# Macaron block with delta-rule attention, one core: sums of squares as TensorE products, and one mixture branch weighted by ScalarE

## The chip, the cores and the metric

One core of a Trainium2 chip. The metric is the device time of one execution in microseconds; the median of three runs of the kernel before is 1182.75 us. Engines: TensorE (PE; its weight loads are listed as PEld), VectorE (DVE), ScalarE (ACT), GpSimd (POOL), SyncE (SP, which issues all the DMAs). A "bank" is one of the eight banks of PSUM, each 128 x 512 f32.

## The reference

Eight sequences of 512 tokens and 256 channels go through half a feed-forward layer, an attention block and half a feed-forward layer again. The change touches the attention: the l2 norms of q and k, and the mixture of four branches.

```python
q = silu(conv(x @ Wq)); k = silu(conv(x @ Wk)); v = silu(conv(x @ Wv))   # 4 heads of 64
beta = sigmoid(x @ Wb)
q, k = q * rsqrt(sum(q*q) + 1e-6), k * rsqrt(sum(k*k) + 1e-6)            # per token and head
# per chunk of 32 tokens: A = -tril(beta k k^T, -1), T = (1 - A)^-1, u = T (beta v), w = T (beta k)
# chunk after chunk: u_i = u - w S; o_i = q S + tril(q k^T) u_i; S += k^T u_i
branches = [fir3(v), fir31(v), delta_o, v]
w = floor_and_renormalise(softmax(gate(x, branches)))                    # 4 weights per token and head
o = sum(w[..., b] * branches[b] for b in range(4))
o = o * rsqrt(mean(o*o) + 1e-5) * onorm_w
x = x + o @ Wo
```

## The kernel before, in words

All work for one sequence is a front part (first feed-forward, projections, convolutions, norms, the inverse T) and a back part (chunk recurrence, gate, mixture, output product, second feed-forward). The kernel is a row of passes that runs the back part of sequence i beside the front part of sequence i+1: one "head" pass (front only), six "body" passes, one "last" pass (like a body without the layernorm of a further sequence) and one "tail" pass (back only). So seven passes hold both parts, eight hold a mixture, and eight hold k and q norms. Each engine has one list of instructions, written out by hand; in a pass, `at.front` and `at.back` pick the parts. Within an engine the order is fixed, so an instruction that waits holds everything behind it.

PSUM banks are handed around by hand. `ORDER` lists, for each kind of pass, which content uses which bank and in which order. TensorE's `claim` waits until the content before in that bank has been given back (`emptied`), the reader's `arrive` waits until the bank is filled, and a reader gives the bank back by raising `emptied`. VectorE's `link` waits for its own instruction, since a later one reads the result.

The steps that the change touches, in the order of a pass:

- ScalarE makes k's two halves by `silu(2)`, `silu(3)` (L632), into `qk_fm` (channels on the partitions). TensorE turns them into banks 0 and 1 (`to_tok`, content `k_t`, L1176). ScalarE squares the two banks into `sq` (L738). VectorE's `k_rows` sums the squares over each head's 64 channels (L1598), adds 1e-6 (L1599), and ScalarE takes the root (L740). Behind the root in ScalarE's list stand `tap(4)`, the four gate gelus (L636), `tap(5)`, the copy of the logits, the copies of k and of the hidden product, and the exponential of the logits (L755).
- TensorE's list after the k transposes: 128 small gram products (`k_products`, L1068, banks 7 and 2), the rest of the q projection, the hidden product, the logit products (L1188), FIR products of the first two heads (`firs(at, 0, ...)`, L1113), the q transposes (`q_t`, banks 3 and 5, L1202), the FIR products of the other two heads.
- ScalarE, after the exponential: `silu(4)`, `silu(5)` (q), copies of the first two FIR banks, the squares of the two q banks (L763), which then are given back.
- VectorE, after the exponential: the mixing weights `mix_w` (L1681 to L1689), then the mixture in place. `f_tok` holds the two FIR branches of a unit (a token tile and head) side by side, `dv_tok` the delta output (slot 0) and v (slot 1). `weighted` multiplies a half of the units, 128 x 1024 elements, by their weights (L1695, four times); `branch_sum` adds `dv_tok` to `f_tok` (L1701, twice), `mixed` adds the two slots (L1706, twice).
- Then the root mean square of the mixed rows: ScalarE squares (L587), VectorE sums (L1711), ScalarE takes the root (L593), VectorE normalises (`mix_normalise`, L1718). TensorE turns the mixed rows (`mixed_rows`, content `mix_t`, banks 6 and 4), with the last FIR products and the v transposes (`v_t`, banks 3 and 5, L1228) between its two halves, then the output product, with the turns of the FIR rows (`fir_rows`) between its halves.
- VectorE after `mix_normalise(1)`: `low_rows(3, "mix_t", 0)` (L1402, the low part of the first mixed rows, which waits for TensorE's turn and ScalarE's high part), `q_rows` (the sum of q's squares, L1617, and the add, L1618), `low_rows(3, "mix_t", 1)`, then the residuals (L1724) and the third layernorm (L1735), whose rows TensorE waits for before the second feed-forward.

The order of the banks that matters here: bank 4 holds the turned beta (`beta_t`) and later the logits, bank 3 in turn a q projection, `q_t`, `v_t`.

## Time and profile before

| | us |
|---|---|
| median of three runs | 1182.75 |
| lowest and highest run | 1180.84, 1190.8 |
| the profiled execution | 1176.66 |
| its span, first to last instruction | 1174.9 |
| TensorE busy | 1051.7 (90%) |
| VectorE busy | 827.4 (70%) |
| ScalarE busy | 551.9 (47%) |
| GpSimd busy | 410.6 (35%) |

The rows further down come from the page and the trace of the profiled execution. A row of a timeline or chain begins with the start in us from the span's start and the time that the row covers; "x8" counts the instructions merged in it; a bracket gives the idle time before and who ended it. A merged row's time runs from the first start to the last end. The ends of matmuls are modelled.

### The profile page before, as it was taken

What the parts mean: (1) busy time and instruction counts of PE and PEld (TensorE: products, weight loads), DVE (VectorE), ACT (ScalarE), POOL (GpSimd) and SP (SyncE); (2) the same over time, 40 slices, a digit from 0 to 9 for tenths busy, and PEclk for the clock granted to TensorE, in tenths of its full rate; (3) what the DMA queues carried; (4) which work ended last, traced back from release to release, by engine and by line L of the source; (5) the groups of instructions that cost most, each with busy time, mean ns of one, the idle gap of its engine ahead of it and who ended that gap; (6) DMA issues with size and microseconds to landing.
All of it is one profiled execution on the core that took longest, in us unless ns stands there. A gap on an engine that the chain in (4) does not pass through costs nothing.

```text
span 1174.9 us, 25682 instructions
## 1 busy us (share of the span) xinstructions
PE 1051.7 (90%) x10348; PEld 785.6 (67%) x10348; DVE 827.4 (70%) x1620; ACT 551.9 (47%) x989; POOL 410.6 (35%) x648
## 2 busy tenths in 40 slices
PE   5858899899999999899998998899998999897738
PEld 4734785588637885488747885488747885486427
DVE  6584478875887668875887668875887668863373
ACT  2254348443564337533575337533574337542431
POOL 7228200951058200961048300771038300770000
PEclk9779799999998999999999999999998999995779
DMA  5140104020130203110140202110040202210000
GB/s 159 20 108 1 37 19 106 4 54 2 51 77 11 45 19 86 24 36 20 33 95 1 55 19 67 42 36 20 28 99 1 54 1 64 46 36 19 1 0 19
DMA packets 82933, 47.45 MB, mean 40 GB/s; under 512 B 58496, under 2 KB 76416, under 8 KB 82816
## 3 DMA queue, kind: packets, MB, share of 16 engines
q1 hardware_dynamic: 82816, 45.82, 16.8%
q8 instruction: 82, 1.34, 0.5%
q14 instruction: 35, 0.29, 0.1%
HBM read 31.12 MB, written 14.68 MB: 39 GB/s over the span
## 4 chain that ended last, share of the span: by engine, by line
PE 69%; DVE 16%; ACT 8%; POOL 3%; issue 3%; DMA 1%; SPq 0%; DVEq 0%; ACTq 0%; POOLq 0%
PE psum L814 14%; PE psum L815 13%; PE psum L816 13%; PE psum L845 6%; DVE arena L1695 4%; PE psum L1007 3%; PE psum L992 3%; PE psum L1026 3%; PE psum L1031 2%; DVE arena L1701 2%; DVE arena L1735 2%; PE psum L1081 2%; PE psum L1188 2%; POOL l_prod L526 1%; POOL arena L530 1%
## 5 line engine op out<-in xcount | busy, mean ns | idle before, releaser
L526 POOL TENSOR_TENSOR l_prod<-arena 64x30 f32<-64x30 f32 (+14 forms) x240 | 143.9, 600 | 547.1 <-DMA arena<-l_dram 528.9
L601 ACT ACTIVATE h_f<-psum,b_col 128x512 f32<-128x512 f32 x128 | 88.1, 688 | 211.7 <-PE psum L816 211.5
L530 POOL TENSOR_TENSOR arena<-arena,l_prod 64x30 f32<-64x30 f32 (+14 forms) x240 | 157.7, 657 | 18.8
L814 PE MATMUL psum<-w_hi,h_hi 128*128 128x256 f32 x512 | 150.4, 294 | 0.0
L1113 PE MATMUL psum<-v_shift,fir_w 128*32 128x512 f32 x1152 | 135.5, 601 | 10.7 <-DVE fir_w L1300 10.7
L815 PE MATMUL psum<-w_lo,h_hi 128*128 128x256 f32 x512 | 144.1, 281 | 0.0
L816 PE MATMUL psum<-w_hi,h_lo 128*128 128x256 f32 x512 | 144.0, 281 | 0.0
L1409 DVE CAST h_hi<-h_f 128x512 fp32r<-128x512 f32 x128 | 63.1, 493 | 86.8 <-ACT h_f L601 43.4
L814 PE MATMUL psum<-xt_hi,w_hi 128*128 128x512 f32 x256 | 113.1, 442 | 7.5 <-DVEq L1396 5.4
L1436 DVE SCALAR_TENSOR_TENSOR conv_acc<-psum,conv_col,conv_acc 128x511 f32<-128x511 f32 x144 | 106.8, 748 | 14.6 <-ACT conv_acc L626 10.9
L845 PE MATMUL psum<-ident,arena 128*128 128x128 f32 x384 | 59.7, 302 | 57.5 <-DVE arena L1735 25.8
L1410 DVE TENSOR_TENSOR h_lo<-h_f,h_hi 128x512 fp32r<-128x512 f32 x128 | 104.9, 820 | 4.4
L815 PE MATMUL psum<-xt_lo,w_hi 128*128 128x512 f32 x256 | 105.9, 414 | 0.0
L816 PE MATMUL psum<-xt_hi,w_lo 128*128 128x512 f32 x256 | 105.2, 411 | 0.0
L814 PEld LDWEIGHTS psum<-w_hi,h_hi 128*128 128x128 f32 x512 | 97.0, 189 | 4.4
L815 PEld LDWEIGHTS psum<-w_lo,h_hi 128*128 128x128 f32 x512 | 97.2, 190 | 2.4
L816 PEld LDWEIGHTS psum<-w_hi,h_lo 128*128 128x128 f32 x512 | 97.0, 189 | 0.0
L845 PEld LDWEIGHTS psum<-ident,arena 128*128 128x128 f32 x384 | 46.9, 153 | 74.2 <-DVE arena L1735 29.5
L1113 PEld LDWEIGHTS psum<-v_shift,fir_w 128*32 128x32 f32 x1152 | 36.7, 111 | 87.8 <-issue 75.8
L814 PEld LDWEIGHTS psum<-xt_hi,w_hi 128*128 128x128 f32 x256 | 51.5, 201 | 20.8 <-issue 10.2
L1485 DVE TENSOR_TENSOR arena<-psum,inv 128x128 f32<-128x128 f32 x64 | 15.6, 285 | 67.4 <-PE psum L1007 67.4
L816 PEld LDWEIGHTS psum<-xt_hi,w_lo 128*128 128x128 f32 x256 | 51.4, 201 | 12.5
(228 smaller groups left out, 2216.3 us busy)
## 6 DMA issues: line engine op xcount, KB each, us to landing
x_in<-in_L_attn_x SPq DMA_DIRECT2D x8, 512.0 KB, 3.9
v_dram<-v_fm SPq DMA_DIRECT2D x16, 256.0 KB, 3.7
v_shift<-v_dram SPq DMA_DIRECT2D x16, 256.0 KB, 3.5
out<-x_tok SPq DMA_DIRECT2D x8, 512.0 KB, 2.8
v_shift<-v_dram SPq DMA_DIRECT2D x16, 255.5 KB, 4.3
v_shift<-v_dram SPq DMA_DIRECT2D x16, 255.0 KB, 5.1
v_shift<-v_dram SPq DMA_DIRECT2D x16, 254.5 KB, 5.7
arena<-in_L_ffn_w SPq DMA_DIRECT2D x2, 1024.0 KB, 7.2
```

Source lines behind the costliest of these rows:

```text
L526: pool.tensor_tensor(prod, l_inv[:, k + 1:, k:k + 1].broadcast_to(shape), l_inv[:, k:k + 1, 0:k].broadcast_to(shape), ALU.mult).then_inc(i ...
L530: pool.tensor_tensor(l_inv[:, k + 1:, 0:k], l_inv[:, k + 1:, 0:k], prod, ALU.add).then_inc(inverted, 1)
L601: act.activation(h_f[:, m % 2, :], bank, ACT.Gelu, bias=b1_col[:, m:m + 1]).then_inc(read, 1)
L814: pe.matmul(dst, a_hi, b_hi, start=first, stop=False, **kw)
L815: pe.matmul(dst, a_hi, b_lo, start=False, stop=False, **kw)
L816: return pe.matmul(dst, a_lo, b_hi, start=False, stop=last, **kw)
L845: last = pe.transpose(bank[:, P * n:P * n + P], src(n), ident[:, :])
L1113: last = pe.matmul(fir[p][0][col:col + 32, :], fir_w[:, group, n - 1 if n else TAPG, :], v_shift[:, group, at_t:at_t + T], start=(n < 2), ...
L1409: link(dve.tensor_copy(h_hi[:, m % RING, :], h_f[:, m % 2, :]))
L1410: dve.tensor_tensor(h_lo[:, m % RING, :], h_f[:, m % 2, :], h_hi[:, m % RING, :].bitcast(F32), ALU.subtract).then_inc(h_split[f], 1)
L1436: ins = dve.scalar_tensor_tensor(out=acc[:, s:], in0=bank[:, 0:T - s], scalar=w[:, CONV - 1 - s:CONV - s], in1=acc[:, s:], op0=ALU.mult, o ...
L1695: return mark(dve.tensor_tensor(src[:, us, :, :], src[:, us, :, :], mix_w[:, us, s:s + 2].unsqueeze(3).broadcast_to([P, 2 * HEADS, 2, D]), ...
```

## The change

The squares of k are taken from `qk_fm`, before any transpose, and so are the squares of q; a 128 x 2 matrix of ones (`pair_sel`) sums them over each head's channels in products whose weights are the squares, eight for k and eight for q. The k sums go into the free columns of the bank of `beta_t`, behind the gram products; the q sums take the place of the q transposes and go into bank 3. VectorE's two sums of squares fall away. In the mixture VectorE weights `dv_tok`'s slot 0 alone, and ScalarE weights slot 1 (v) in sixteen activations of 128 x 64, eight for each half, ahead of and behind the first two FIR copies; VectorE's `branch_sum` waits for them.

```diff
--- before.py
+++ after.py
@@ -120,6 +120,7 @@
         t_two = v_shift[D:D + CHUNK, 6, 32:WIDE].rearrange("p (u j) -> p u j", j=CHUNK)
         f_fm = sb("f_fm", [P, HEADS, T])
         beta_fm = sb("beta_fm", [32, T])
+        pair_sel = sb("pair_sel", [P, 2])
         rows_tok = sb("rows_tok", [P, 3, UNITS])
         nrm, inv = sb("nrm", [P, 2, UNITS]), sb("inv", [P, 2, UNITS])
         c1, c2n = sb("c1", [P, UNITS]), sb("c2n", [P, UNITS])
@@ -154,7 +155,8 @@
         taps_l = f_fm[:, 0, 0:GROUPS * (LONG + 1)].rearrange("p (g n) -> p g n", g=GROUPS)
         taps_s = f_fm[:, 1, 0:GROUPS * CONV].rearrange("p (g n) -> p g n", g=GROUPS)
         at_flat = at_tok[:, :, :].rearrange("p u i -> p (u i)")
-        q_sq = at_flat[:, 0:TILES * C].rearrange("p (u d) -> p u d", u=UNITS)
+        k_sq = sq[:, :, :]
+        q_sq = at_flat[:, 0:HALVES * T].rearrange("p (h t) -> p h t", h=HALVES)
         stat_sel = at_flat[0:D, 0:4 * BR * P].rearrange("p (b m) -> p b m", m=P)
         mean_sel = v_fm[0:D, 1, 0:2 * P].rearrange("p (a m) -> p a m", a=2)
         stat_all = v_fm[:, 1, 2 * P:4 * P].rearrange("p (a m) -> p a m", a=2)
@@ -179,7 +181,7 @@
         K = [("k", (0, 1)), ("beta", (4,)), ("q", (3, 5)), ("beta_t", (4,)), ("k_t", (0, 1)), ("gram", (7, 2)), ("hidden", (6,))]
         LOGIT = [("logit", (4,)), ("logit_t", (4,))]
         FIR = [("fir", (7, 2, 0, 1))]
-        Q = [("q_t", (3, 5))]
+        Q = [("q_sum", (3,))]
         MIX = [("mix_t", (6, 4)), ("wo", (7, 2))]
         V_T = [("v_t", (3, 5)), ("f_t", (0, 1, 6, 4)), ("lhalf", (3, 5)), ("at0", (7, 2))]
         FFN_C = [("ln3", (6, 4)), ("upc", (0, 4) * (KT // 2)), ("outc", (1, 6))]
@@ -307,6 +309,8 @@
         hm_made = sem("hm_made")
         lshift_made = sem("lshift_made")
         exp_made = sem("exp_made")
+        mix_w_made = sem("mix_w_made")
+        v_weighted = sem("v_weighted")
         mix_made = sem("mix_made")
         mix_squared = sem("mix_squared")
         onrm_made = sem("onrm_made")
@@ -318,8 +322,8 @@
         dve_step = sem("dve_step")
         INV_STEPS = 2 * (CHUNK - 2) + 2
         T_LOADS = CPT + 2 * (CPT - 1)
-        DVE_STEPS = {"head": 43, "body": 78, "last": 73, "tail": 40}
-        CONST_MADE, C_LOADED, SETUP_DVE = 60, 57, 36
+        DVE_STEPS = {"head": 41, "body": 75, "last": 70, "tail": 39}
+        CONST_MADE, C_LOADED, SETUP_DVE = 63, 57, 36
         ZEROED, IDENT_MADE = 5, 7
         SETUP_UP, SETUP_FFN, SETUP_PROJ, SETUP_LARGE, SETUP_FIR = 2, 5, 9, 13, 29
 
@@ -467,7 +471,7 @@
                                     pattern=[[-1, P]], channel_multiplier=1))
             assert made == IDENT_MADE
             for t, v in ((low_strict[:, :], 1.0), (up_incl[:, :], 1.0), (eye32[:, :], 0.0), (x_t[:, :, :], 0.0),
-                         (stat_sel, 0.0), (mean_sel, 0.0), (head_mask, 0.0)):
+                         (stat_sel, 0.0), (mean_sel, 0.0), (head_mask, 0.0), (pair_sel[:, :], 0.0)):
                 make(pool.memset(t, v))
             pool.wait_ge(xn_made[0], 1)
             for t, v in ((v_shift[:, :, :], 0.0), (ms_tok[:, :, :], 0.0), (mx_tok[:, :, :], 0.0)):
@@ -483,6 +487,7 @@
             for half in range(2):
                 part = slice(D * half, D * half + D)
                 make(pool.memset(mean_sel[:, half, part], 1.0 / D))
+                make(pool.memset(pair_sel[part, half:half + 1], 1.0))
 
             for par in range(2):
                 for st in range(2):
@@ -656,6 +661,12 @@
                     act.wait_ge(du_ready, TILES * i + t + 1)
                     act.activation(du[:, :, :, :], psum[:, 5:7, 0:HALVES * D].rearrange("p a (h d) -> p a h d", h=HALVES),
                                    ACT.Copy).then_inc(du_made, 1)
+
+                def weight_v(b):
+                    act.wait_ge(mix_w_made, i + 1)
+                    for u in range(2 * HEADS * b, 2 * HEADS * b + 2 * HEADS):
+                        last = act.activation(dv_tok[:, u, 1, :], dv_tok[:, u, 1, :], ACT.Identity, scale=mix_w[:, u, 3:4])
+                    last.then_inc(v_weighted, 1)
 
                 def s_copy(t):
                     act.wait_ge(s_ready, (TILES - 1) * i + t + 1)
@@ -733,9 +744,9 @@
                     out_of(at, "beta", 0, beta_fm[:, :], ACT.Sigmoid, src=lambda b: b[0:32, :])
                     silu(2)
                     silu(3)
-                    for t in range(2):
-                        bank, _ = arrive(act, at, "k_t", t)
-                        act.activation(sq[:, t, :], bank, ACT.Square).then_inc(kq_squared, 1)
+                    for h in range(HALVES):
+                        act.wait_ge(silu_made, 6 * j + 3 + h)
+                        act.activation(k_sq[:, h, :], qk_fm[:, h, 0, :], ACT.Square).then_inc(kq_squared, 1)
                     act.wait_ge(nrm_made, j + 1)
                     act.activation(nrm[:, 0, :], nrm[:, 0, :], ACT.Sqrt).then_inc(kqroot_made, 1)
                     tap(4)
@@ -756,14 +767,16 @@
                 if at.front:
                     silu(4)
                     silu(5)
+                    for h in range(HALVES):
+                        act.wait_ge(silu_made, 6 * j + 5 + h)
+                        act.activation(q_sq[:, h, :], qk_fm[:, h, 1, :], ACT.Square).then_inc(kq_squared, 1)
+                if at.back:
+                    weight_v(0)
+                if at.front:
                     for h in range(2):
                         out_of(at, "fir", h, f_fm[:, h, :])
-                    for t in range(2):
-                        bank, read = arrive(act, at, "q_t", t)
-                        act.activation(at_flat[:, 512 * t:512 * t + 512], bank, ACT.Square).then_inc(kq_squared, 1)
-                        act.wait_ge(kq_squared, 4 * j + 3 + t)
-                        act.sem_inc(read, 1)
-                if at.back:
+                if at.back:
+                    weight_v(1)
                     mix_square(at, 0)
                     mix_root(at, 0)
                     mix_square(at, 1)
@@ -1053,8 +1066,25 @@
                 bank, full = claim(pe, at, "beta_t")
                 pe.sem_inc(passed, 1)
                 for t in range(TILES):
-                    last = pe.transpose(bank[:, 32 * t:32 * t + 32], beta_fm[:, P * t:P * t + P], ident[0:32, 0:32])
-                last.then_inc(full, 1)
+                    pe.transpose(bank[:, 32 * t:32 * t + 32], beta_fm[:, P * t:P * t + P], ident[0:32, 0:32])
+
+            def square_sums(cols, squares):
+                for t in range(TILES):
+                    for h in range(HALVES):
+                        first = HEADS * t + 2 * h
+                        last = pe.matmul(cols[:, first:first + 2], squares[:, h, P * t:P * t + P], pair_sel[:, :],
+                                         start=True, stop=True)
+                return last
+
+            def k_sums(at):
+                bank, full = where(at, "beta_t")
+                pe.wait_ge(kq_squared, 4 * at.j + 2)
+                square_sums(bank[:, TILES * 32:TILES * 32 + UNITS], k_sq).then_inc(full, 1)
+
+            def q_sums(at):
+                bank, full = claim(pe, at, "q_sum")
+                pe.wait_ge(kq_squared, 4 * at.j + 4)
+                square_sums(bank[:, 0:UNITS], q_sq).then_inc(full, 1)
 
             def k_products(at):
                 grams = [claim(pe, at, "gram", b) for b in range(2)]
@@ -1175,6 +1205,7 @@
                     pe.wait_ge(silu_made, 6 * j + 4)
                     to_tok(at, "k_t", lambda h: qk_fm[:, h, 0, :])
                     k_products(at)
+                    k_sums(at)
                     projection(at, "q", 1, 1)
                     bank, full = claim(pe, at, "hidden")
                     for k in range(HALVES):
@@ -1198,8 +1229,7 @@
                     turn(at, "logit_t", 0, lambda t: lg_fm[:, P * t:P * t + P])
                 if at.front:
                     firs(at, 0, range(1, 9))
-                    pe.wait_ge(silu_made, 6 * j + 6)
-                    to_tok(at, "q_t", lambda h: qk_fm[:, h, 1, :])
+                    q_sums(at)
                     pe.wait_ge(v_shifted[1], 64 * j + 64)
                     firs(at, 1, range(0, 8))
                     if not at.back:
@@ -1591,12 +1621,10 @@
                 def k_rows():
 
                     bank, read = arrive(dve, at, "beta_t")
+                    dve.tensor_scalar(nrm[:, 0, :], bank[:, TILES * 32:TILES * 32 + UNITS], 1e-6, None, ALU.add).then_inc(nrm_made, 1)
                     link(dve.tensor_copy(rows_tok[:, 1, :].rearrange("p (t h) -> p t h", t=TILES),
                                          bank[:, 0:TILES * 32].rearrange("p (t h) -> p t h", t=TILES)[:, :, 0:HEADS]))
                     dve.sem_inc(read, 1)
-                    dve.wait_ge(kq_squared, 4 * j + 2)
-                    link(dve.tensor_reduce(rows_tok[:, 0, :], sq_u, AX.X, ALU.add))
-                    dve.tensor_scalar(nrm[:, 0, :], rows_tok[:, 0, :], 1e-6, None, ALU.add).then_inc(nrm_made, 1)
                     dve.wait_ge(kqroot_made, j + 1)
                     link(dve.reciprocal(inv[:, 0, :], nrm[:, 0, :]))
                     link(dve.tensor_tensor(c1[:, :], rows_tok[:, 1, :], inv[:, 0, :], ALU.mult))
@@ -1613,9 +1641,10 @@
                                       low_strict[:, :].unsqueeze(1).broadcast_to([P, UNITS, CHUNK]), ALU.mult).then_inc(l_made, 1)
 
                 def q_rows():
-                    dve.wait_ge(kq_squared, 4 * j + 4)
-                    link(dve.tensor_reduce(rows_tok[:, 2, :], q_sq, AX.X, ALU.add))
-                    dve.tensor_scalar(nrm[:, 1, :], rows_tok[:, 2, :], 1e-6, None, ALU.add).then_inc(qnrm_made, 1)
+                    bank, read = arrive(dve, at, "q_sum")
+                    dve.tensor_scalar(nrm[:, 1, :], bank[:, 0:UNITS], 1e-6, None, ALU.add).then_inc(qnrm_made, 1)
+                    dve.wait_ge(qnrm_made, j + 1)
+                    dve.sem_inc(read, 1)
 
                 def q_inverse():
                     dve.wait_ge(qroot_made, j + 1)
@@ -1686,17 +1715,22 @@
                                            .broadcast_to([P, TILES, HEADS * BR]), ALU.max))
                     link(dve.tensor_reduce(lsum[:, :], lg[:, :, :], AX.X, ALU.add))
                     link(dve.reciprocal(linv[:, :], lsum[:, :]))
-                    link(dve.tensor_tensor(mix_w[:, :, :], lg[:, :, :], per_row(linv[:, :], BR), ALU.mult))
+                    dve.tensor_tensor(mix_w[:, :, :], lg[:, :, :], per_row(linv[:, :], BR), ALU.mult).then_inc(mix_w_made, 1)
+                    dve.wait_ge(mix_w_made, i + 1)
 
                     units = [slice(2 * HEADS * b, 2 * HEADS * b + 2 * HEADS) for b in range(2)]
 
                     def weighted(src, s, b):
                         us = units[b]
-                        return mark(dve.tensor_tensor(src[:, us, :, :], src[:, us, :, :],
-                                                      mix_w[:, us, s:s + 2].unsqueeze(3).broadcast_to([P, 2 * HEADS, 2, D]), ALU.mult))
+                        branches = slice(0, 2) if src is f_tok else slice(0, 1)
+                        count = branches.stop
+                        return mark(dve.tensor_tensor(src[:, us, branches, :], src[:, us, branches, :],
+                                                      mix_w[:, us, s:s + count].unsqueeze(3).broadcast_to([P, 2 * HEADS, count, D]),
+                                                      ALU.mult))
 
                     def branch_sum(b, made):
                         us = units[b]
+                        dve.wait_ge(v_weighted, 2 * i + b + 1)
                         dve.wait_ge(dve_step, made)
                         return mark(dve.tensor_tensor(f_tok[:, us, :, :], f_tok[:, us, :, :], dv_tok[:, us, :, :], ALU.add))
```

## Rows read from the trace of the kernel before

**Rows 1.** The page, part 1: engine, busy us, share of span, instructions

```profile
PE 1051.7 (90%) x10348; PEld 785.6 (67%) x10348; DVE 827.4 (70%) x1620; ACT 551.9 (47%) x989; POOL 410.6 (35%) x648
```

**Rows 2.** Waits of TensorE, whole run: us in total, times, longest

```profile
PE psum L845 <- DVE arena L1735: 25.8, 16, 3.9
PE psum L845 <- DVE arena L1718: 21.4, 8, 12.5
...
PE psum L915 <- DMA x_t<-tt_dram: 1.7, 1, 1.7
```

**Rows 3.** Chain that ended last, 566 to 632 us: start, us, what

```profile
591.11 1.09 ACT arena L738 x2
...
592.22 1.23 DVE rows_tok L1598
...
593.69 0.02 ACT nrm L740
...
601.74 1.28 ACT L755
...
604.97 0.29 DVE mix_w L1689
...
624.81 0.70 DVE x_tok L1724
```

**Rows 4.** Timeline of TensorE, 572 to 632 us: start, us, what, idle before

```profile
592.65 0.50 PE L814 MATMUL psum<-xt_hi,wqkv_hi 128*128 128x512 f32 x1
...
596.66 2.36 PE L1188 MATMUL psum<-f_fm,w2g_pad 128*32 128x512 f32 x7 [0.94 <-ACT f_fm L636]
...
617.43 0.65 PE L845 MATMUL psum<-ident,arena 128*128 128x128 f32 x4 [1.37 <-DVE arena L1718]
...
619.01 1.09 PE L845 MATMUL psum<-ident,v_fm 128*128 128x128 f32 x8
```

**Rows 5.** Timeline of weight loads (PEld) at 565 us, of products at 589 us

```profile
565.31 0.98 PEld L992 LDWEIGHTS psum<-hm,x_t 128*128 128x128 f32 x8
...
589.27 0.43 PE L1056 MATMUL psum<-ident,beta_fm 32*128 32x32 f32 x4
```

**Rows 6.** ScalarE: timeline in the head; all of L643, ns min/median/max

```profile
107.34 3.94 ACT L643 ACTIVATE v_shift<-arena,c 128x64 f32<-128x64 f32 x16
...
L643 ACT ACTIVATE v_shift<-arena,c x128: 332/336/408, 107.3 to 1047.0; 128x64 f32<-128x64 f32 x128
```

**Rows 7.** Timeline of ScalarE, 572 to 632 us

```profile
604.61 1.15 ACT L632 ACTIVATE qk_fm<-conv_acc 128x512 f32<-128x512 f32 x2
608.08 1.08 ACT L605 ACTIVATE f_fm<-psum 128x512 f32<-128x512 f32 x2 [2.32 <-PE psum L1113]
```

**Rows 8.** Timeline of VectorE, 572 to 632 us

```profile
605.28 4.25 DVE L1695 TENSOR_TENSOR arena<-arena,mix_w 128x1024 f32<-128x1024 f32 x3
...
612.31 0.99 DVE L1706 TENSOR_TENSOR arena<-arena 128x512 f32<-128x512 f32 x1
613.23 1.53 DVE L1701 TENSOR_TENSOR arena<-arena 128x1024 f32<-128x1024 f32 x1
...
616.57 0.81 DVE L1718 TENSOR_TENSOR arena<-arena,oinv 128x512 f32<-128x512 f32 x1
...
619.62 0.68 DVE L1402 TENSOR_TENSOR xt_lo<-psum,xt_hi 128x512 fp32r<-128x512 f32 x1
620.22 1.21 DVE L1617 TENSOR_REDUCE rows_tok<-at_tok 128x16 f32<-128x1024 f32 x1
```

**Rows 9.** Stretches: length, busy us of five engines, PEclk, DMA share, GB/s

```profile
67.00:71.40 4.40, 3.88 (x138) 3.39 (x139) 1.40 (x2) 3.14 (x6) 0.00 (x0) 0.61 0.59 132
...
361.00:369.00 8.00, 6.79 (x31) 5.33 (x32) 3.62 (x7) 2.50 (x4) 7.11 (x12) 0.57 0.00 0
...
1026.00:1034.00 8.00, 4.85 (x35) 3.83 (x36) 4.63 (x11) 3.37 (x5) 7.06 (x13) 1.00 0.00 1
```

**Rows 10.** Timeline of VectorE in the tail

```profile
1126.16 1.22 DVE L1695 TENSOR_TENSOR arena<-arena,mix_w 128x1024 f32<-128x1024 f32 x1
```

## The prediction

> **What bounds the kernel now.** I read the page first: TensorE is busy 90% of the span [rows 1]. So what counts is where TensorE still stands, and the waits by engine say it: over all passes it stands 25.8 us for the third layernorm's rows (L1735), 21.4 us for the mixed rows (L1718), far more than the inverse's transfer, 1.7 us [rows 2]; in one pass it is 0.94 us before the logit products and 1.37 us before the mixed rows [rows 4]. Then the chain of waits for one pass (566 to 632 us; a pass is 133 us): from 590 to 617 us it runs through ScalarE and VectorE, not TensorE. The k transposes go to ScalarE's squares at 591.11, to VectorE's sum at 592.22, to the root of the k norms at 593.69; behind that root ScalarE's queue holds tap, gelus, logit copy and the exp table at 601.74; then VectorE's mixing weights at 604.97 and the mixture; from 617.4 TensorE runs on until VectorE takes output 1 at 624.81 [rows 3]. So a pass gets longer by what the root of the k norms is late, less what the mixture gains, plus whatever holds TensorE between 617 and 625 us.
>
> **The k sums.** Gone: ScalarE's wait for the transposes, and VectorE's sum of 1.23 us [rows 3]. New: eight products, each with 128x128 of squares as weights and 2 columns. The four products of a tile step at L992, 4-byte as well, are 8 loads [rows 5], so I count 16 instructions. Their price is not in the trace. The upper bound has the same weights and 64 columns: 8 loads start within 0.98-0.19 = 0.79 us, 0.11 us each (0.19 is one load's own duration). The lower is the turn of beta, weights only 32 rows deep, a transpose: 4 in 0.43 us, of which the last one's 0.22 is latency, 0.07 each [rows 5]. 16 times these: 1.8 or 1.1 us. I take 1.8, as the weights have the same size; the v transposes, with twice the columns of L992, also start 0.14 us apart at most (8 in 1.09 us [rows 4]), so it isn't the columns that set it.
> They stand behind the 128 gram products, which end where the q projection starts, 592.65 [rows 4]. The squares, made on ScalarE from the silu output, are ready by 591.5 and not waited for. 592.65+1.8 = 594.45, some 0.1 to land, 0.2 for VectorE's add: the root at 594.75 for 593.69, **1.06 us later** (0.4 with 1.1 us). VectorE's saved sum buys nothing here, since the sums now wait for TensorE's queue. TensorE's own 1.8 us lies in its 0.94 us stand and under the later gelus.
> By the Trainium skill (TensorE: Matmul & The Clock Gate, section "Back-to-back issue gap") a product of up to 64 columns starts every 25 ns, and the 16 would take 0.4 us; the same page's section on LDWEIGHTS goes by the weights' columns, 107 ns for 128, so 1.7 us. The 0.11 us of [rows 5] sides with the second. With the first the root would come 0.35 us early, a pass be as long as before, and the run take 1181, an estimate to which I give 0.03.
>
> **The mixture.** s is the root's start. Before, the mixing weights are ready at s+11.56, three weightings follow in 4.25 us (1.42 each), and branch sum 1 ends at 613.23+1.53 = 614.76, s+21.07 [rows 3, 8]. After: the d slot alone, half the elements; by the 512-element product at 0.81 and half of 1.42, 0.71, I take 0.72 [rows 8]; twice, that saves 1.4 us. ScalarE: its two silus end at 605.76, s+12.07 [rows 7]; two q squares of the same shape, 1.15 more; then 8 weightings. The form has run in the head, 16 in 3.94 us, one lasting 0.34, so 0.24 from start to start [rows 6]; 8 take 2.02, done s+15.25. VectorE wants them at s+11.56+1.42+0.72+1.42 = s+15.1. Then the two fir copies (1.08) [rows 7] and 8 more, done s+18.3; wanted at s+18.4, after branch sum 0 (1.53 less some overlap, 1.46), the second half weighting and the first mixing (0.99) [rows 8]. So ScalarE is just in time, 0.15 us lost: branch sum 1 ends at s+19.8, **1.25 us better** within the pass. The fir copies, now behind the weightings, free banks 7 and 2, wanted by the output products some 10 us later: nothing; without that cover they would cost their 2 us.
>
> **The q sums and bank 3.** TensorE's eight q transposes (1.09 us, as the v transposes [rows 4]) become 16 instructions at 0.11, 1.8 us: 0.75 more. It ended its fir products at 617.43-1.37 = 616.06, s+22.4 [rows 4], and now does at s+23.1: it goes straight on to the mixed rows, the 1.37 us stand is gone, and half of the mixture's gain is unused. But the q sums lie in bank 3, which the v transposes claim next, and it is given back by VectorE's q rows, which stand behind the second normalise and the low part of the mixed rows. Before, ScalarE's q squares gave it back soon after the fir copies of 608.08 [rows 7], and the v transposes ran at once, at 619.01 = s+25.32 [rows 4]. VectorE's low part starts at 619.62 and its next one at 620.22 [rows 8], 5.46 us after branch sum 1. After: s+19.8+5.46, plus the add and its signal (0.17+0.15): v transposes at **s+25.6**. TensorE, ready at s+23.1+1.6, stands some 0.8 us, with mixed rows 1, output and f rows queued behind. A faster VectorE would not remove it, as its low part waits for the mixed rows' transposes.
> The q reduction of 1.21 us [rows 8] is gone, but from the v transposes to 624.81 the path is TensorE's own, 5.8 us, and does not shrink. Per pass: 1.06+(25.6-25.32) = **1.3 us later**, seven times: 9.1.
>
> **Head, tail, rest.** In the head the k root stands before the inverse, on whose transfer the first merge waits (1.7 us, once [rows 2]), so its delay counts whole. The mean clock there is 0.61 [rows 9]: the 16 take between 1.8 and 3.6 us, the root is 1.1 to 2.9 us late, I take 1.8 (with cheap products 0.7). In the other passes that transfer is not waited for, so a later inverse costs nothing. The tail has only the mixture: 1.22 us for 1024 elements [rows 10], two halves save 1.2, ScalarE is free and in time: -1.1. The three memsets stand in the set-up, under TensorE's first feed-forward: nothing. Sum: 9.1+1.8-1.1 = +9.8 us. The profiled execution, 1176.66 us (span 1174.9), would take 1186.5; the median of the runs, 1182.75, is 0.5% above it, and the same step gives **1192.5**.
>
> **Rivals.** A, the above. Its own range: the low clock behind the layernorm wait differs by pass (0.57 over eight us at 361, 1.00 at 1026 [rows 9]), 3.4 us lost or none; seven passes shifted anew make some 4 us either way: 1188 to 1197.
> B, narrow products are cheap, 1.1 us or less. At 1.1: root 0.4 late, v transposes still held by bank 3, 0.7 a pass, 4.9, head 0.9, tail -1.1: 1187.4. At half of that the root is 0.15 early: 0.15 a pass, 1183. So 1182 to 1188, in the middle 1185. For it: only 2 columns; against: rows 5.
> C, faster: bank 3 is free in time. With cheap products (root 0.2 late) and VectorE's add done before TensorE ends fir slot 8, the mixture's 1.25 us reaches the v transposes: 1.05 us a pass earlier, with head and tail -7.7: 1175. For it: VectorE loses 3.8 us of work a pass. Against: its order, low part ahead of q rows. It decides where the q add ends before s+24.1.
> D, slower: ScalarE becomes the bound of the mixture. If its 16 weightings start 0.34 us apart, their own duration, not 0.24, the second eight end 1.6 us later, and branch sum 1, bank 3 and the v transposes with them: 11 us more, 1203.7. It decides from 0.25 us each on. For it: there is no slack. Against: rows 6.
>
> **How the numbers follow.** A 0.55, B 0.2, C 0.08, D 0.17. About 1% (11.8 us) is what a measurement can tell, as three runs of before lie between 1180.84 and 1190.8. Slower by over 1%, past 1194.6: D, and a third of A: 0.36. Faster by over 1%, below 1170.9: C with a kind clock, 0.04. Within: 0.60. The range leaves out C and most of D: 1182 to 1201; A's alone is 1188 to 1197.
>
> **What would show it.** The 16 k products some 0.11 us apart behind the grams, VectorE idle some 3 us before the k add, the k root 2.1 us behind the end of the grams; no stand before the mixed rows and a new one of 0.7 to 1 us before the v transposes, released by VectorE's q add; VectorE waiting 0.2 us or less for ScalarE's weightings. I am wrong if the products start every 0.03 to 0.06 us (B), if there is no stand at the v transposes (C), if VectorE waits over 0.5 us for a weighting (D), or if the period of a pass grows by under 0.5 or over 2.5 us.

## The result: slower by 2.2%, and the profile after

| | before | after |
|---|---|---|
| median of four runs beside each other, us | 1183.62 | 1209.49 |
| lowest and highest run after | | 1206.25, 1216.05 |
| ratio, 95% interval | | 1.0216 [1.0153, 1.028] |
| span of the profiled execution | 1174.9 | 1209.2 |

The change costs 25.9 us; I had forecast 1192.5 and a range that ended at 1201. A "stand" is a stretch in which TensorE does nothing. First part 1 of the page after, then the waits of TensorE (engine and line, what it waited for: us in total, times, longest; "DVEq" is a signal that VectorE's queue gives between its instructions).

```profile
PE 1089.7 (90%) x10540; PEld 822.0 (68%) x10540; DVE 798.9 (66%) x1604; ACT 581.9 (48%) x1117; POOL 401.0 (33%) x651
```

```profile
PE psum L858 <- DVE arena L1769: 24.5, 15, 3.1
PE psum L858 <- DVE arena L1752: 12.3, 2, 11.4
PE psum L1098 <- issue: 9.5, 4, 2.6
...
PE psum L858 <- DVEq L1647: 6.4, 7, 1.4
```

Against [rows 1], VectorE has 28.5 us less work and TensorE 38 us more busy time. Against [rows 2], the stand before the mixed rows (L1752, before L1718) is gone from the passes and 11.4 of 12.5 us are left in the tail; the stand before the v transposes is there (L1647 gives bank 3 back, behind VectorE's q add in L1645), 6.4 us over seven passes. The third line is one that I had no term for: 9.5 us in four pieces inside the gram products (L1098), with no releaser. The windows cut at the first merge product of each pass (from head to tail) tell which passes. After:

```profile
0.00:134.80 134.80, 97.80 (x746) 73.01 (x747) 75.50 (x142) 45.48 (x78) 68.52 (x140) 0.82 0.30 71
134.80:273.91 139.11, 131.63 (x1313) 99.32 (x1313) 97.57 (x196) 71.08 (x138) 42.78 (x68) 0.95 0.17 39
273.91:408.10 134.19, 128.79 (x1313) 96.65 (x1312) 96.83 (x197) 71.88 (x139) 47.99 (x73) 0.99 0.17 40
408.10:546.83 138.73, 131.52 (x1314) 99.02 (x1313) 97.03 (x197) 71.84 (x139) 47.50 (x73) 0.95 0.17 39
546.83:680.93 134.10, 128.78 (x1313) 96.56 (x1312) 96.68 (x197) 71.88 (x139) 48.00 (x73) 0.99 0.18 40
680.93:817.20 136.27, 129.43 (x1313) 97.76 (x1313) 96.79 (x197) 71.90 (x139) 47.59 (x73) 0.97 0.17 40
817.20:952.75 135.55, 129.97 (x1313) 97.50 (x1312) 97.03 (x197) 71.78 (x139) 48.09 (x73) 0.97 0.18 40
952.75:1089.88 137.13, 127.75 (x1287) 96.18 (x1287) 91.05 (x177) 69.09 (x134) 46.67 (x73) 0.94 0.15 32
1089.88:1209.23 119.35, 84.00 (x636) 66.05 (x636) 50.40 (x110) 36.99 (x72) 3.81 (x5) 0.68 0.03 10
```

And before, cut in the same way:

```profile
0.00:128.80 128.80, 90.96 (x723) 66.15 (x724) 78.90 (x144) 45.68 (x78) 68.61 (x137) 0.84 0.31 74
...
264.23:397.55 133.32, 127.39 (x1290) 94.69 (x1289) 100.44 (x199) 68.04 (x123) 48.78 (x73) 0.97 0.18 41
...
663.74:796.48 132.74, 125.83 (x1289) 94.38 (x1288) 100.50 (x199) 68.12 (x123) 49.59 (x73) 0.97 0.18 41
...
1058.30:1174.94 116.64, 79.22 (x636) 63.12 (x636) 51.38 (x110) 33.07 (x56) 3.81 (x5) 0.75 0.03 10
```

The columns are length, the busy times of five engines, granted clock, DMA share, GB/s. Passes 2, 4 and 6 after, without a stand in the gram products, are 0.9, 1.1 and 2.0 us longer than the same passes before (1.3 forecast); passes 1, 3, 5 and 7 have the stands, 136.3 to 139.1 us and a lower mean clock. Of the 34.3 us between the spans, 25.6 lie in passes 1 to 7, 6.0 in the head, 2.7 in the tail; they are more than the 25.9 us of the medians because the profiled execution before lies 7.0 us below its median and the one after 1.5 above. TensorE's timeline after shows pass 2 beside pass 3 (L1098 are the gram products, L1075 the k sums, L827 the q projection):

```profile
334.53 1.29 PE L1098 MATMUL psum<-qk_fm 64*32 64x32 f32 x128
335.75 1.95 PE L1075 MATMUL psum<-pair_sel,arena 128*128 128x2 f32 x16
337.56 0.48 PE L827 MATMUL psum<-xt_hi,wqkv_hi 128*128 128x512 f32 x1
...
468.66 1.14 PE L1098 MATMUL psum<-qk_fm 64*32 64x32 f32 x111
471.96 0.30 PE L1098 MATMUL psum<-qk_fm 64*32 64x32 f32 x17 [2.16 <-issue]
472.19 2.32 PE L1075 MATMUL psum<-pair_sel,arena 128*128 128x2 f32 x16
```

In pass 3 the same list stops for 2.16 us after 111 of the 128 gram products, and the k sums, which wait in the same queue, start 3.53 us after the first gram product instead of 1.22 and take 2.32 us for 1.95. The root behind them is late by both. Behind it the granted clock is at half, 1.2 GHz; windows of pass 3, then of pass 2 at the same place:

```profile
466.80:473.60 6.80, 3.93 (x151) 3.51 (x150) 1.99 (x4) 3.10 (x5) 0.00 (x0) 1.00 0.45 106
473.60:480.40 6.80, 6.80 (x21) 4.74 (x24) 4.87 (x12) 5.21 (x8) 0.00 (x0) 0.50 0.10 39
333.20:340.00 6.80, 6.50 (x163) 5.85 (x164) 3.18 (x10) 4.62 (x7) 0.00 (x0) 1.00 0.40 105
340.00:346.80 6.80, 6.37 (x39) 2.11 (x41) 5.55 (x9) 6.21 (x11) 0.00 (x0) 1.00 0.47 101
```

Who stops TensorE in the middle of a list that waits for nothing? The DMA view (queue, kind: packets, MB, share of 16 engines) of pass 3, 469.4 to 474.4 us, then of pass 2, 334.4 to 339:

```profile
q8 instruction: 2, 0.03, 2.7%
...
q8 instruction: 1, 0.02, 1.5%
```

And the same queue in part 3 of the page:

```profile
q8 instruction: 84, 1.38, 0.5%
```

This queue moves no tensor but instructions: 84 fetches of 16.4 KB for 10540 products and as many loads, one for 251 of them (82 in the kernel before, for 2 x 10348: 252). With the 472 other records that the trace has for TensorE (470 of them instructions on semaphores) it is one for 256.6. So they are TensorE's own code. By the Trainium skill (Trainium Architecture — The Big Picture, section "The software stack") an instruction has 64 bytes, which would make a fetch 256 of them, an estimate that the count bears out; that the code is brought in when the program is loaded, as the same section of the Trainium skill says, the trace contradicts with these 84 fetches during the execution. Smaller windows tell the order: in pass 3 a first fetch falls between 469.4 and 470.9, where TensorE stops, a second only between 472.9 and 474.4; in pass 2 the first falls between 335.9 and 337.4, when the gram products are through (335.8).

My theory from here: **the gram products run through 256 instructions in 1.2 us, faster than code arrives when they begin late in a block of it, and now the k root hangs behind them.** The experiments test it. Before, a stand of that kind was there too, in pass 5 (timeline of TensorE before):

```profile
724.33 1.12 PE L1068 MATMUL psum<-qk_fm 64*32 64x32 f32 x109
727.90 0.31 PE L1068 MATMUL psum<-qk_fm 64*32 64x32 f32 x19 [2.45 <-issue]
```

But that pass is no longer than the others, 132.74 us: its root came from ScalarE and VectorE, and the 0.9 us stand at the logits that passes 2, 3, 4, 6 and 7 have ([rows 4] shows pass 4's) is gone from it.

### The profile page after: what moved, and what is told of

It is laid out like the page before. It is cut to its first block, busy times and chain, and to the rows that moved or that the text cites. A ratio compares the mean times of both kernels' runs of the same rounds, so it can differ in the third digit from the quotient of the medians.

```text
span 1209.2 us, 26189 instructions
## 1 busy us (share of the span) xinstructions
PE 1089.7 (90%) x10540; PEld 822.0 (68%) x10540; DVE 798.9 (66%) x1604; ACT 581.9 (48%) x1117; POOL 401.0 (33%) x651
## 3 DMA queue, kind: packets, MB, share of 16 engines
q1 hardware_dynamic: 82816, 45.82, 16.4%
## 4 chain that ended last, share of the span: by engine, by line
PE 71%; DVE 13%; ACT 7%; issue 4%; POOL 3%; DMA 1%; SPq 0%; DVEq 0%; POOLq 0%; ACTq 0%
PE psum L827 14%; PE psum L828 13%; PE psum L829 13%; PE psum L858 6%; PE psum L1020 3%; PE psum L1005 3%; PE psum L1039 2%; PE psum L1044 2%; PE psum L1111 2%; PE psum L1075 2%; DVE arena L1735 2%; DVE arena L1727 2%; DVE arena L1769 2%; POOL l_prod L531 1%; PE psum L1219 1%
## 5 line engine op out<-in xcount | busy, mean ns | idle before, releaser
L535 POOL TENSOR_TENSOR arena<-arena,l_prod 64x30 f32<-64x30 f32 (+14 forms) x240 | 150.1, 625 | 18.8
L827 PE MATMUL psum<-w_hi,h_hi 128*128 128x256 f32 x512 | 149.7, 292 | 0.0
L827 PE MATMUL psum<-xt_hi,w_hi 128*128 128x512 f32 x256 | 112.6, 440 | 7.4 <-DVEq L1426 5.8
L1466 DVE SCALAR_TENSOR_TENSOR conv_acc<-psum,conv_col,conv_acc 128x511 f32<-128x511 f32 x144 | 106.8, 748 | 15.3 <-ACT conv_acc L631 11.6
L1439 DVE CAST h_hi<-h_f 128x512 fp32r<-128x512 f32 x128 | 58.3, 456 | 87.7 <-ACT h_f L606 43.3
L1440 DVE TENSOR_TENSOR h_lo<-h_f,h_hi 128x512 fp32r<-128x512 f32 x128 | 102.3, 799 | 4.4
L827 PEld LDWEIGHTS psum<-w_hi,h_hi 128*128 128x128 f32 x512 | 96.4, 188 | 4.5
L827 PEld LDWEIGHTS psum<-xt_hi,w_hi 128*128 128x128 f32 x256 | 51.4, 201 | 20.4 <-issue 9.9
```

The source lines that it names most:

```text
L535: pool.tensor_tensor(l_inv[:, k + 1:, 0:k], l_inv[:, k + 1:, 0:k], prod, ALU.add).then_inc(inverted, 1)
L827: pe.matmul(dst, a_hi, b_hi, start=first, stop=False, **kw)
L1439: link(dve.tensor_copy(h_hi[:, m % RING, :], h_f[:, m % 2, :]))
L1440: dve.tensor_tensor(h_lo[:, m % RING, :], h_f[:, m % 2, :], h_hi[:, m % RING, :].bitcast(F32), ALU.subtract).then_inc(h_split[f], 1)
L1466: ins = dve.scalar_tensor_tensor(out=acc[:, s:], in0=bank[:, 0:T - s], scalar=w[:, CONV - 1 - s:CONV - s], in1=acc[:, s:], op0=ALU.mult, o ...
```

## The experiments

All are the changed kernel with one edit or, in e7, e9 and e11, two; but e4 and e10 are the kernel before with one part of the change. Each ratio is to executions of the kernel before taken beside that run. Stands are those of over 1 us inside gram products or k sums.

| | edit | median us | ratio to before | passes with a stand |
|---|---|---|---|---|
| after | | 1209.5 | 1.0216 [1.0153, 1.028] | 1, 3, 5, 7 |
| e1 | 32 products more in the head (64 instructions with their loads) | 1194.75 | 1.0106 [1.0066, 1.0145] | none |
| e8 | 64 products more (128 instructions) | 1196.96 | 1.0111 [1.0065, 1.0157] | 2, 6 |
| e2 | k sums ahead of the grams | 1191.24 | 1.0075 [1.0044, 1.0105] | none |
| e3 | q add earlier on VectorE | 1195.26 | 1.0113 [1.0077, 1.0149] | 1, 5, 7 |
| e7 | e2 and e3 | 1186.72 | 1.0028 [1.0002, 1.0053] | none |
| e11 | e1 and e3 | 1185.68 | 1.0009 [0.9987, 1.0031] | none |
| e5 | q norms as before | 1194.38 | 1.0094 [1.0059, 1.0128] | 1, 3, 6 |
| e10 | k sums alone, on before | 1199.8 | 1.0111 [1.0068, 1.0154] | 1, 3, 6 |
| e6 | k norms as before | 1180.51 | 0.9972 [0.9947, 0.9998] | 1 |
| e9 | e6 and e3 | 1181.57 | 0.9975 [0.9953, 0.9998] | 1, 4, 7 |
| e4 | mixture alone, on before | 1182.15 | 0.9976 [0.9946, 1.0007] | 5 |

### Where the stands come from: e1 and e8

```diff
                     bank, full = claim(pe, at, "hidden")
+                    if not at.back:
+                        for _ in range(32):     # e8: 64
+                            pe.matmul(bank[:, 0:64], wh_hi[:, 0, :], xt_hi[:, 0, 0:64], start=True, stop=True)
```

The products are overwritten by the hidden product; apart from their own time in the head, they only move everything behind them within the blocks. A "place", in the expectation for e8 and further on, is the number of an instruction in TensorE's list, counted from 0 and modulo 256.

> The changed kernel, with 32 narrow dummy products (64 instructions) in the head, where TensorE waits for VectorE anyway: every later instruction stands a quarter of a 256-instruction block further on in TensorE's code. Theory S (stands): the four stands of 2.2 to 2.6 us inside the gram products come from a code block that isn't there yet, and since the k sums stand behind the grams, the root and all of the pass is late by them, with the half clock that follows. By the count of instructions no gram section then starts late in a block: no such stand in any of the seven passes, no half clock between the grams and the FIR products, 1189 to 1196 us. Rival C (clock): the 16 narrow products let the clock fall by themselves, stands or not: half clock behind them in four or more passes, 1203 us or more.

> The changed kernel with 64 more narrow products in the head, ahead of the hidden product and overwritten by it: 128 instructions, half a block of 256, where the run with 32 products shifted TensorE's list by a quarter block. Theory (stands at block borders inside the gram products, each with half the clock behind it): the gram products now begin at places 111, 233, 99, 221, 87, 209, 75 of their blocks in passes 1 to 7; stands of over 2 us came at 203 and above so far and none at 169 and below, so they should now be in passes 2, 4 and 6, and none in 1, 3, 5 and 7. Three stands at (1209.5 - 1194.8)/4 = 3.7 us each on top of 1194.8: 1206, at least 1202. Rival (the additional products in the head help by themselves, as work that keeps TensorE busy there): about 1195 again, or less.

TensorE's waits of e1 have no line for the gram products (at most 0.6 us at the k sums, once), and the run is **14.7 us faster than the changed kernel, with work added**. In e8 the stands are back, in passes 2 and 6, which had none in the kernel after, and gone from 1, 3, 5 and 7:

```profile
PE psum L1098 <- issue: 4.7, 2, 2.5
```

So where the stands come goes by the place in the code and not by the added work. The times alone don't say so: e8's median is within the noise of e1's, nearer to the rival's 1195 than to my 1206. Two points of the expectation for e8 failed. Pass 4, beginning at place 221, did not stand: a fetch came ahead of its gram products (between 599.4 and 601.4 us; they begin at 602.1), not into them. And 1197 is below the 1202 that I called the least: passes 2 and 6 are 136.75 and 136.80 us against 134.0 in passes 3 and 5, so a stand cost 2.8 us there, not 3.7. Between the profiled executions of the kernel after and e1, passes 1, 3, 5 and 7 are together 15.3 us shorter, passes 2, 4 and 6 together 2.9 longer, and the head 3.9 shorter.

The traces settle what the stand waits for. Counting all of TensorE's records (loads, products, semaphores), the gram products of pass 3 after begin at place 227, and the stand comes after 111 products of two instructions each: 227 + 222 = 449, which is place 193 of the next block. Pass 1 has 239 + 210, pass 5 215 + 234, pass 7 203 + 246: 449 each time. All 20 stands of the table, the one in pass 5 before, and the stands of 1.5 us that before and e4 have in the q projection of pass 1 lie at place 193, and the product behind each of them starts 2.3 to 2.5 us after a fetch on queue 8 began. Pair the first fetch of a run with the second place 193 of its list, the second with the third, and so on: in 1071 pairs over all thirteen traces, no instruction at place 193 starts less than 2.28 us after the start of its fetch. **The stand is the wait for that fetch.**

### What hangs on them: e2, e6 and e9

e2:

```diff
-                    k_products(at)
                     k_sums(at)
+                    k_products(at)
```

> The changed kernel, with the k sums ahead of the gram products. Theory S: the root comes as early as in the kernel before (within 0.3 us of 62.8 us from the merge's start) in all passes, stands in the grams remain in one or two passes but no longer delay the root, the pass is some 0.3 us longer than before from the wait for bank 3: 1186 to 1193 us. Rival C: half clock behind the sums in four or more passes as in the changed kernel, 1203 us or more.

e6 puts ScalarE's squares of the transposes and VectorE's sum back (the diff of the change, backwards, for k alone); e9 has e3's edit too.

> The changed kernel with the k norms as before (transposes squared, summed by VectorE); q sums and mixture stay changed. Theory: the root hangs on ScalarE and VectorE again and not on the gram products, so that stands inside those (by the count of instructions in passes 1, 4 and 7) cost nothing on the path: root 62.8 us after the merge. What is left is bank 3, +0.3 us a pass or 2, the tail -1.1, the head as before: 1183 to 1188. Rival (a stand inside the gram products costs the same whatever hangs on them): 3 x 3.7 more, 1194 to 1199.

> The kernel with the k norms as before, the q sums and the mixture changed, and in addition the q add moved right behind the first normalise. Theory: root as before, no stand at the v transposes (0.65 to 1.2 us in each of seven passes of the run without the move), so 1180.5 - 5.5 = 1175, between 1173 and 1177, faster than before by 0.6 to 0.9%. Rival (gains ahead of the third layernorm's wait come back as half clock behind it): the half clock of a pass grows from 3.4 to 6.8 us and the time stays at 1179 to 1182.

e6 took the whole loss away, 29 us (1180.5, below the 1183 to 1188 that I expected), but had its stand in pass 1 alone, so it could not tell what a stand costs there. (In its pass 4 a fetch came between 592.2 and 594.2, ahead of the gram products; in e9's pass 4 it did not, though TensorE's list is the same.) e9 could: TensorE's waits, a pass with the stand in its timeline, and the windows of that pass (4) between two without one:

```profile
PE psum L1099 <- issue: 6.4, 3, 2.4
```

```profile
596.78 1.17 PE L1099 MATMUL psum<-qk_fm 64*32 64x32 f32 x114
599.81 0.29 PE L1099 MATMUL psum<-qk_fm 64*32 64x32 f32 x14 [1.85 <-issue]
```

```profile
403.14:536.23 133.09, 128.31 (x1298) 95.73 (x1297) 98.69 (x198) 71.99 (x139) 47.49 (x73) 0.97 0.18 41
536.23:669.38 133.15, 127.26 (x1297) 95.64 (x1297) 96.15 (x198) 71.93 (x139) 47.89 (x73) 0.97 0.17 41
669.38:802.36 132.98, 128.20 (x1298) 95.70 (x1297) 97.82 (x198) 71.92 (x139) 47.87 (x73) 0.97 0.18 41
```

A stand of 1.85 us, and the pass is as long as its neighbours; pass 7, with a stand of 2.4 us, is 129.67 us long against 129.44 in e6, where it has none. (Pass 1 of e9, 138.66 us, says nothing: its gram products already begin 4.3 us later than in the other passes.) The roots show why. Counted from the first merge product of a pass, the root starts at 62.8 to 62.9 us in passes 2 to 7 before; after, at 64.0 in 2, 4 and 6 and at 66.7, 66.6 and 68.5 in 3, 5 and 7; in e9 at 62.8 in all six, stand or not. **The stand costs only where the root hangs on the gram products.**

In e2 the root does not hang on them either (62.8 to 62.9), and it gains 18.3 us, to 1191.2 as expected. But that run can't tell whether the moved root or the missing stands made the gain, since it has no stand of over 1 us: its gram products begin 32 places later, so that by the count passes 5 and 7 should have had one, but the fetch began ahead of them there, and at place 193 TensorE stood 0.6 us at most. And in e2 and e7 the clock falls without a stand: in e7, built like e2, it is at half over the sums and gram products of pass 3 (457.0 us on).

```profile
457.00:463.80 6.80, 6.75 (x143) 5.67 (x143) 4.52 (x12) 5.21 (x8) 0.00 (x0) 0.50 0.11 41
```

### The k sums alone: e10 and e5

e10 takes from the change only the lines for k; e5 those for k and the mixture.

> The kernel before with the k sums alone behind the gram products (q norms and mixture as before). Theory: 1.1 us a pass for the later root, 7.7; some 2.5 us for each of the stands that fall into the gram products, by the count in passes 1 and 6, 5; the head 2: 1184 + 15 = 1199, between 1195 and 1203. Rival (the k sums cost little by themselves, and it is their meeting with the other two parts that costs): 1185 to 1191.

> The changed kernel with the q norms as before (transposes, squares, VectorE's sum); k sums and mixture stay changed. Theory: root 1.1 us late in every pass, no stand before the v transposes, the mixture's 1.2 us makes up for the root; stands inside the gram products where they begin at place 203 or above, by the count in passes 1 and 6, cost 3.7 us each, the head +4: 1183.6 + 2 x 3.7 + 4 - 1 = 1194, between 1190 and 1198. Rival (the k sums cost only their own 1.9 us a pass, 1.1 net, and the stands are the q sums' doing): 1185 to 1189 with no stand in any pass.

```profile
PE psum L1089 <- issue: 4.6, 2, 2.6
...
PE psum L1066 <- issue: 1.4, 1, 1.4
```

Those are e10's waits: stands in the gram products (L1089) of passes 1 and 6, the ones counted out beforehand, and 1.4 us in the k sums of pass 3 (L1066), which I had not counted out; it is at place 193 too, and e5 has the same one. Both times came out as the theory had them, 1199.8 for 1199 and 1194.4 for 1194, which with three stands for two, and intervals of 4 to 5 us to either side, is luck in part. The k sums alone, stands included, cost 15 us by the medians (13 by the ratio).

### Bank 3: e3, e7 and e11

```diff
                     mix_normalise(0)
+                    if at.front:
+                        q_rows()
                     mean_square(1)
...
-                if at.front:
+                if at.front and not at.back:
                     q_rows()
```

> The changed kernel, with VectorE's q rows moved ahead, right behind the first normalise, so that bank 3 is given back before TensorE has turned the first mixed rows. Theory S: the stand of 0.7 to 1.4 us before the v transposes goes in all seven passes, the four stands in the grams stay: 1202 to 1205 us. Rival: the stand covers a wait that comes anyway (for the mixed rows or the layernorm): 1208 to 1211 us.

> The changed kernel with both moves: k sums ahead of the gram products, and the q add behind the first normalise instead of behind the low part. Theory: root as before (62.8), no stand before the v transposes, so what remains of the change is the mixture's gain and the head: 1191.2 less 0.7 us x 7 = 1186, between 1183 and 1189; if all gains reached the end, 1175. Rival (what is gained ahead of the third layernorm's wait comes back as half clock behind it, and a pass stays near 133.2 us): 1189 to 1192, no better than the sums ahead alone.

> The changed kernel with the 32 additional products in the head (no stand in the gram products) and the q add moved behind the first normalise (no stand before the v transposes). Theory: both stands are separate terms, so 1194.8 - 0.7 x 7 = 1190, between 1187 and 1192, of which the root's 1.1 us a pass is what is left of the change. Rival (the move repairs the same loss as the shifted blocks, as its run gained 14 us where 5.6 were foreseen): no further gain, 1193 to 1197.

In all three TensorE's waits have no line for the q add any more. e3 gained 14 us, far over the 5 to 7 foreseen. By accident pass 3 lost its stand as well (138.7 us to 133.5): a fetch came ahead of the gram products there (462 to 464 us; they begin at 464.6). That is 5.2 us; another 4.1 lie in pass 7, which kept its stand and had a mean clock of 0.96 for 0.94, and 2.9 in the head. e7 came out as expected, 1186.7 for 1186. e11 has neither stand, and is not measurably slower than before; it gained 9.1 us on e1 for some 5, and so fell below the 1187 to 1192 expected. Windows of two passes of e1, then of the same ones of e11:

```profile
538.36:673.57 135.21, 129.90 (x1313) 97.44 (x1312) 96.86 (x197) 71.88 (x139) 48.11 (x73) 0.97 0.17 40
673.57:807.59 134.02, 128.70 (x1313) 96.59 (x1312) 96.74 (x197) 71.87 (x139) 48.01 (x73) 0.99 0.17 40
```

```profile
535.74:668.98 133.24, 128.70 (x1314) 96.58 (x1313) 97.11 (x197) 71.80 (x139) 47.56 (x73) 0.99 0.17 41
668.98:802.38 133.40, 128.47 (x1314) 96.42 (x1313) 97.72 (x197) 71.84 (x139) 47.63 (x73) 0.99 0.17 40
```

The stand itself is 0.6 us (134.02 to 133.40); the first pair shows 2.0 because e1's pass also has a longer stretch of half clock (0.97). In e6 to e9 the same edit went the other way, no gain:

```profile
400.56:533.88 133.32, 126.96 (x1298) 94.85 (x1297) 98.19 (x198) 71.88 (x139) 48.30 (x73) 0.99 0.17 41
```

That is e6's pass 3; e9's is the first of its three windows above. TensorE is 1.35 us more busy in e9 at a lower mean clock, and the pass only 0.2 us shorter: what the stand (1.1 us in e6's pass 3) gave went into half clock, as the rival expected.

### The mixture alone: e4

e4 adds `weight_v` to the kernel before, ahead of the fir copies and behind the q squares of the transposes, and halves VectorE's `dv_tok` weighting.

> The kernel before, with the mixture part of the change alone: ScalarE weights v in sixteen activations, the norms of k and q as before. TensorE's code is the same as before. Theory S: ScalarE is in time, branch sum 1 ends 1.2 us earlier in a pass, TensorE's stand before the mixed rows (1.1 to 1.4 us) goes, the tail is 1.1 us shorter: 1173 to 1178 us. Rival: ScalarE is late, VectorE waits for the weightings by 1 us or more a pass: 1183 us or more.

```profile
PE psum L857 <- DVE arena L1735: 15.7, 8, 11.4
```

The stand before the mixed rows fell from 21.4 to 15.7 us [rows 2], but no gain can be measured (the interval holds 1). Part of it VectorE now loses waiting for the weightings, which stand behind the q squares in ScalarE's list (its waits; L665 is `weight_v`):

```profile
DVE arena L1718 <- ACT arena L665: 4.4, 7, 1.6
```

The 1173 to 1178 that I expected failed. e4's pass 5 has a stand in the gram products, on which its root does not hang, and is the shortest of passes 1 to 6 (131.24 us).

## Why the prediction was wrong

The mechanism was right where TensorE ran undisturbed. Pass 2 after, in the chain of waits:

```profile
335.82 1.89 PE psum L1075 x16
337.71 0.02 issue
337.73 0.18 DVE nrm L1624
...
337.94 0.02 ACT nrm L751
...
363.48 1.53 PE psum L858 x12
```

- **The k sums.** 16 products in 1.89 us (forecast 1.8), the root 2.2 us behind the start of the first (335.75; 2.1). B, cheap products, was wrong. By the table of the Trainium skill (TensorE: Matmul & The Clock Gate, section "Back-to-back issue gap"), 25 ns for a product of up to 64 columns by itself, they would have taken 0.4 us, an estimate. The same section says that in a stream of loads and products both set the spacing, and the trace agrees: the 16, each with its own load, start 0.113 us apart.
- **The mixture.** ScalarE's weightings take 2.00 and 2.01 us (2.02), VectorE does not wait for them (its waits name L668 in no pass), and branch sum 1 ends at 357.79, 19.85 us behind the root (19.8). D was wrong.
- **Bank 3.** The q add starts at 363.20, 25.3 behind the root, and the v transposes at 363.48, 25.5 behind it (25.6); C was wrong. Summed, the forecast without a stand in the gram products was +9.8; e1, the run without one, has +10.6. Its interval goes from +8 to +17 us, so a match to within 1 us is in part luck.

The timeline of VectorE in that pass carries this,

```profile
356.27 1.52 DVE L1735 TENSOR_TENSOR arena<-arena 128x1024 f32<-128x1024 f32 x1
...
363.20 0.17 DVE L1645 TENSOR_SCALAR nrm<-psum 128x16 f32<-128x16 f32 x1
```

and that of ScalarE:

```profile
350.96 2.00 ACT L668 ACTIVATE arena<-arena,mix_w 128x64 f32<-128x64 f32 x8
...
353.82 2.01 ACT L668 ACTIVATE arena<-arena,mix_w 128x64 f32<-128x64 f32 x8
```

**The step that failed is "They stand behind the 128 gram products, which end where the q projection starts, 592.65".** I read that end in one pass and used it in all. It is not fixed: in passes 1, 3, 5 and 7 after, the gram products end 2.2 to 2.6 us later, and the root with them. That could have been seen: the stand of 2.45 us in pass 5 of the trace before was there to be read, and I dropped it because it cost nothing then. Moving the root behind a stretch of TensorE makes every stand in that stretch a stand of the path. With four passes hit, e1's difference says 14.7 us, 3.7 each: some 2.4 for the stand, the rest, I take it, half clock behind it. That the 48 instructions more in a pass moved the gram products to a worse place is part of the same miss: 10348 to 10540 products stood in the diff, but I counted only their time.

My own range, 1188 to 1197, allowed for the clock and not for stands: e1, without them, lies in it (1194.75). But the clock moves as much as the edits do: e11 gets 9 us from a 5 us stand, e9 nothing.

**Head and tail.** The head's +1.8 is neither borne out nor refuted: heads with the k sums range from 130.9 to 135.3 us over the runs (nine, three of them with added products; mean 133.2), heads without them from 128.8 to 131.4 (four, mean 130.6), a difference of 2.6 with a spread that is larger. What made the head after take 134.8 is not shown. The tail's -1.1 came in the stand (12.5 to 11.4), but the tail after is 2.7 us longer at a mean clock of 0.68 for 0.75; it is 116.6 in e8 at 0.70, whose tail is the same, and 121.4 in e10, whose tail is that of before, so this is the clock of an execution and not the change.

**What stays open.** What decides whether the fetch comes ahead of the gram products or into them, since e6 and e9 have the same list on TensorE and differ in it. What decides whether the stretch of half clock behind the layernorm's wait is a short or a long one. The count alone does not say which passes will stand: e1's none and e5's and e10's 1 and 6 came as counted, but of e8's three only two, of e6's three only one, of e2's two none of over 1 us. And what a stand costs on the path is known only roughly, 2.8 us in e8 and 3.7 by e1.

## What to carry to other kernels

When a dependency is moved from one engine's queue behind work of another, look at that work in every pass, its stands "for nothing" included; a stand that cost nothing becomes a term. Hundreds of tiny products in a row are a place where such stands arise; whether they strike depends on the count of all instructions before, and on when the fetch begins, so time a change in two positions (a few dozen instructions shifted) before you judge it. Here that was worth 13 to 15 us of the 26. As for this change: the k sums are the loss, and the other two parts without them are within 0.3% of before (e6, e9), barely faster.

## What the runs showed of the hardware that I had not expected

TensorE can stand 2.2 to 2.6 us in the middle of a list without any semaphore, until 2.3 to 2.5 us after queue 8 began to fetch 16.4 KB of code; 64 instructions more in the head made the run 1.2% faster than the changed kernel. Behind such a stand its granted clock was at half for 6.8 us in pass 3. And each of the eight k sums, with two columns and 128 x 128 weights of 4 bytes, is two pairs of load and product, 0.113 us a pair from start to start. Against the 0.11 us of [rows 5] with 64 columns, the columns hardly count.
